# Value products two spots later in the attention loop, opening instructions reordered, and 80 small identity products on TensorE

## The chip, the core and the metric

The kernel runs on one core of a Trainium2 chip. Its engines run side by side, each through its own list of instructions in order, and wait for one another at semaphores: TensorE (PE, matmuls into PSUM), VectorE (DVE), ScalarE (ACT), GpSimd (POOL) and SyncE (SP, which here only issues DMAs). The metric is the device time of one execution in microseconds (us). A profile adds the span of the instructions and the clock that TensorE was granted, 1.00 for 2.4 GHz and 0.50 for 1.2 GHz.

## The reference

Two layers, each with a cross attention and a mixture-of-experts feed-forward, over 8 batches of 128 rows and 256 columns. The change touches the first attention only:

```
x = x + xattn0(layernorm(x), ctx, ctx, encoding, Wq, bq, Wk, bk, Wv, bv, Wm, bm)
  q, k, v = (W @ input + bias) for each batch, 16 heads of 8 channels
  q, k    = rotary(q), rotary(k)            # t * f0 + rotate_half(t) * f1
  prob    = softmax(q k^T / sqrt(8))        # per head, 256 x 256
  out     = Wm @ (prob v) + bm
x = x + ffn0(layernorm(x));  x = x + xattn1(layernorm(x), ctx);  x = x + ffn1(layernorm(x))
```

## The kernel before

**Layout.** In the first attention a "block" b is a batch (NB = 8), and a block has 16 heads, taken as 8 pairs (PAIRS). q and k of a block are split into three bf16 parts, written to DRAM, and read back as "stacks" qstk and kstk, in which both heads of a pair lie one above the other in 64 rows each. The largest score of every row has to be known before the exponentials. So each pair is multiplied twice: once for the row maxima (max_scores, L506, reduced by VectorE at L1175 into mx), and, when the negated maxima have been put into rows of qstk, once more for the exponentials (scores, L527, then ScalarE's Exp at L884 into a prob buffer). pv (L542) multiplies two pairs' prob with the values vt; a block has four such groups (QUADS).

**The way of the maxima.** When the four pairs of a half block are reduced, POOL negates them and splits them into bf16 (negate, six small operations, L1060 to L1064); TensorE transposes them (max_transpose, "maxT", L514), VectorE copies them out (mT, L1179), and SP sends them into qstk (L410).

**The way of q and k.** For block b+3, project (L491) makes q and k; VectorE multiplies with the rotary table (factors, "rope", L1164). Then POOL adds the two (rotate, L337), ScalarE copies the first bf16 part (L891), POOL subtracts (rest, L340), ScalarE copies the second part (L895), POOL makes the third (third, L343), and SP writes and reads back the stacks. POOL's list in block b is: divide(b-1), negate of (b+1, first half), rotate, rest, normalize(b+4), third, negate of (b+1, second half).

**The order.** A block has 16 "spots", two for each pair. All engines follow the same written order: a_uses(b, spot) lists what uses the shared PSUM banks misc(u) in a spot. Even spots hold scores for the next pair and max_scores of a pair of block b+1 or b+2 (MAXES). MAXT says where the maxT stand (6 and 14 in most blocks). q stands at spot 1, k at 5, and v+wm (values of the next block, L497, and output of the last one, L550) at 9; pv at 3, 7, 11 and 15. On VectorE flip (transposes the pv bank, pvT, L1189, and takes the reciprocals, L1191) is at spot 1, flip_back (L1198) at 6. POOL's divide (L1085) stands between the two. In block 7 VectorE also computes the statistics of the next layernorm between flip and flip_back.

**The banks.** misc(u) is one of three banks in turn: max_scores takes two, every other use one. A use may start when the use three banks back has been read (misc_free). exp_buf holds two pairs of scores, prob has three buffers, and pv's bank is one, which flip must have read (pv_free) before the first pv of the next block.

**The opening.** PROLOGUE is the written order before block 0: k and q of blocks 0 to 2, the maxima of block 0, its first maxT. TensorE there waits for the first stacks to come from DRAM (stack_in). VectorE's statistics of blocks 2 to 7 (norm_stats, bn_stats L1150) stand behind q of block 1.

## Time and profile before

| | us |
|---|---|
| median of 3 runs | 462.84 |
| lowest, highest | 459.05, 464.03 |
| the profiled execution | 462.08 |
| its span | 460.3 |
| TensorE busy, VectorE busy | 368.5, 325.0 |
| ScalarE busy, POOL busy | 175.2, 65.9 |
| mean granted clock | 0.915 |

The span is the time from the first to the last instruction of the profiled execution, and 1.8 us lie around it. Busy time is summed over stages that have different limits, so the rows below are read stage by stage. A row of the timeline holds one or several equal instructions; the bracket at its end is the idle time of the engine before it, and what ended that.

### The profile page before, as it was taken

To read this page: it belongs to the slowest core of one execution; us is meant where nothing else is said; L and a number is where in the kernel's file an instruction comes from. 1 tells how busy PE (TensorE), PEld (TensorE's weight loads), DVE (VectorE), ACT (ScalarE), POOL (GpSimd) and SP (SyncE) were. 2 spreads that over 40 slices of the span, in tenths; PEclk is the share of its full clock that TensorE was granted. 3 is DMA by queue.
4 is the path that set the end of the run, shared out by engine and by line. 5 is a ranking of instruction groups with operands and counts; after the bars stand their busy time and mean duration, and the time that the engine had idled before them with its cause. 6 is when DMAs were issued, how large, how long until landed. Compare 5 with 4: busy or idle time off the path is not lost.

```text
span 460.3 us, 7585 instructions
## 1 busy us (share of the span) xinstructions
PE 368.5 (80%) x2754; PEld 221.3 (48%) x2754; DVE 325.0 (71%) x890; ACT 175.2 (38%) x237; POOL 65.9 (14%) x154
## 2 busy tenths in 40 slices
PE   3264888887776669999999999999777887396895
PEld 3122434443343233666666676666455555253453
DVE  5886788989887654674555357677877667869684
ACT  1102456655656512334333334343444444342001
POOL 1214344644422000000000000110011111100000
PEclk9855799999999889999999999999989778976999
DMA  7482366786520400000000000505045444630011
GB/s 244 136 257 69 94 202 160 228 246 216 153 71 19 147 0 0 1 0 2 0 0 1 0 0 3 160 15 146 0 140 155 143 115 129 187 99 0 1 47 46
DMA packets 62371, 41.81 MB, mean 91 GB/s; under 512 B 3968, under 2 KB 60160, under 8 KB 62336
## 3 DMA queue, kind: packets, MB, share of 16 engines
q1 hardware_dynamic: 58240, 34.55, 25.6%
q10 hardware_dynamic: 4096, 6.79, 4.6%
q8 instruction: 22, 0.36, 0.4%
q14 instruction: 13, 0.11, 0.1%
HBM read 26.71 MB, written 14.42 MB: 89 GB/s over the span
## 4 chain that ended last, share of the span: by engine, by line
PE 51%; DVE 33%; issue 7%; POOL 4%; ACT 2%; DMA 2%; DVEq 0%; ACTq 0%; POOLq 0%
PE psum L644 14%; PE psum L631 14%; DVE mx L1175 7%; PE psum L719 4%; PE psum L491 3%; PE psum L619 3%; DVE rope_ab L1164 2%; PE psum L542 2%; DVE stats L1150 2%; PE psum L506 2%; PE psum L757 2%; DVE rs_a L1139 2%; DVE rs_a L1138 1%; PE psum L827 1%; PE psum L843 1%
## 5 line engine op out<-in xcount | busy, mean ns | idle before, releaser
L1175 DVE TENSOR_REDUCE mx<-psum 128x2 f32<-128x512 f32 x128 | 81.1, 683 | 12.8 <-PE psum L506 11.4
L884 ACT ACTIVATE prob<-psum 128x1024 f32<-128x1024 f32 x64 | 63.9, 1022 | 48.7 <-PE psum L527 48.7
L1380 DVE SCALAR_TENSOR_TENSOR xall<-psum,comb,xall 128x256 f32<-128x256 f32 x128 | 53.1, 478 | 41.5 <-PE psum L644 41.1
L644 PE MATMUL psum<-wdn,act 128*128 128x256 f32 x320 | 75.5, 379 | 0.7 <-DVE xall L1377 0.7
L631 PE MATMUL psum<-xnT,wup 128*128 128x512 f32 x160 | 75.6, 596 | 0.0
L644 PEld LDWEIGHTS psum<-wdn,act 128*128 128x128 f32 x320 | 60.7, 190 | 25.9 <-issue 19.1
L946 ACT ACTIVATE rel<-psum 128x512 f32<-128x512 f32 x40 | 23.9, 597 | 95.5 <-PE psum L631 95.5
L343 POOL TENSOR_TENSOR parts<-qk_rest,parts 128x512 bf16<-128x512 f32 x15 | 17.3, 1156 | 226.0 <-ACT parts L972 223.4
L506 PE MATMUL psum<-kstk,qstk 64*128 64x256 bf16 x256 | 27.8, 299 | 22.3 <-DVE mx L1175 12.1
L1002 ACT ACTIVATE prob<-psum 128x1024 f32<-128x1024 f32 x32 | 32.6, 1024 | 25.4 <-PE psum L741 25.4
L542 PE MATMUL psum<-prob,vt 128*32 128x256 f32 x512 | 36.7, 399 | 5.8 <-ACT prob L884 4.7
L631 PEld LDWEIGHTS psum<-xnT,wup 128*128 128x128 f32 x160 | 29.9, 192 | 22.3 <-issue 20.6
L506 PEld LDWEIGHTS psum<-kstk,qstk 64*128 64x128 bf16 x256 | 9.9, 98 | 35.7 <-DVE mx L1175 23.6
L527 PE MATMUL psum<-qstk,kstk 64*128 64x256 bf16 x256 | 25.4, 284 | 0.6 <-DMA qstk<-mT 0.5
L948 ACT ACTIVATE act<-rel 128x512 f32<-128x512 f32 x40 | 25.2, 630 | 1.3
L757 PE MATMUL psum<-prob,vt 128*32 128x128 f32 x512 | 24.5, 321 | 0.2 <-ACT prob L1002 0.2
L542 PEld LDWEIGHTS psum<-prob,vt 128*32 128x32 f32 x512 | 16.5, 112 | 14.5 <-ACT prob L884 6.2
L619 PE MATMUL psum<-eye,xn 128*128 128x128 f32 x48 | 11.9, 341 | 9.7 <-DVE xn L1158 8.1
L827 PE MATMUL psum<-wd,xnT 128*128 128x512 f32 x32 | 16.9, 677 | 2.8 <-DVE xall L1421 2.8
L527 PEld LDWEIGHTS psum<-qstk,kstk 64*128 64x128 bf16 x256 | 8.5, 96 | 21.6 <-issue 13.7
L757 PEld LDWEIGHTS psum<-prob,vt 128*32 128x32 f32 x512 | 14.4, 124 | 7.6 <-issue 5.0
L741 PE MATMUL psum<-qstk,kstk 64*128 64x128 bf16 x256 | 13.6, 232 | 4.4 <-issue 2.4
(156 smaller groups left out, 469.1 us busy)
## 6 DMA issues: line engine op xcount, KB each, us to landing
qstk<-stack_scratch SPq DMA_DIRECT2D x32, 256.0 KB, 4.1
kstk<-stack_scratch SPq DMA_DIRECT2D x30, 256.0 KB, 4.5
stack_scratch<-parts SPq DMA_DIRECT2D x31, 192.0 KB, 2.1
stack_scratch<-parts SPq DMA_DIRECT2D x33, 128.0 KB, 2.1
wup<-in_wup ACTq DMA_DIRECT2D x4, 640.0 KB, 4.8
wdn<-in_wdn ACTq DMA_DIRECT2D x4, 640.0 KB, 5.9
stack_scratch<-parts SPq DMA_DIRECT2D x33, 64.0 KB, 1.9
out<-xall SPq DMA_DIRECT2D x8, 128.0 KB, 1.7
```

Of the source, the lines that this page charges most:

```text
L506: last = nc.tensor.matmul(banks[s][:, nb * D:(nb + 1) * D], qstk[par][rows, pair, nb * P:(nb + 1) * P], kstk[par][rows, pair, :], start=Tr ...
L527: last = nc.tensor.matmul(exp_buf(k)[:, s, mb * D:(mb + 1) * D], kstk[b % SETS][rows, k, mb * P:(mb + 1) * P], qstk[b % SETS][rows, k, :], ...
L542: last = nc.tensor.matmul(pv_bank(1)[32 * j:32 * j + 32, g * D:(g + 1) * D], vt[b % 2][:, mb, 4 * t + j, 8:40] if low else vt[b % 2][:, mb ...
L619: last = nc.tensor.transpose(bank[:, n * P:(n + 1) * P], blk, eye[:])
L631: last = nc.tensor.matmul(psum[:, n % 2, :], wup[:, f, BLOCKS[g], :], xnT[:, f, c * HALF:(c + 1) * HALF], start=(f == 0), stop=(f == 1))
L644: last = nc.tensor.matmul(y_banks(y)[:, j // 2, (j % 2) * D:(j % 2 + 1) * D], act2[n % 2][:, j * P:(j + 1) * P], wdn[:, BLOCKS[g], :], sta ...
L757: last = nc.tensor.matmul(pv_bank(k // 2)[32 * j:32 * j + 32, g * P:(g + 1) * P], v[:, 8 * k + h, 8:40], prob[k % 2][:, at * P:(at + 1) * ...
L884: nc.scalar.activation(prob[(b * PAIRS + k) % 3][:], exp_buf(k).rearrange("p a n -> p (a n)"), ACT.Exp, scale=SCALE).then_inc(exp_done, 1)
L948: nc.scalar.activation(act2[n % 2][:], rel[n % 2][:], ACT.Square).then_inc(a_done, 1)
L1002: nc.scalar.activation(prob[k % 2][:], exp_buf(k).rearrange("p a n -> p (a n)"), ACT.Exp, scale=SCALE).then_inc(exp_done, 1)
L1175: nc.vector.tensor_reduce(mx[:, half, :, 4 * s + p4:4 * s + p4 + 1], bank.rearrange("n (b m) -> n b m", b=2), AX_X, ALU.max).then_inc(misc ...
L1380: last = nc.vector.scalar_tensor_tensor(out=xall[:, b, :], in0=src, scalar=comb[:, b, e:e + 1], in1=xall[:, b, :], op0=ALU.mult, op1=ALU.add)
```

## The change

It has five parts.

1. pv of a group is issued two spots later on TensorE, at spots 5, 9 and 13 and at spot 1 of the next block, and the last one behind the loop. prob has four buffers, since a group's prob is now read later.
2. With it q goes from spot 1 to 3, k from 5 to 7, v+wm from 9 to 11, flip from 1 to 3, flip_back from 6 to 8, and in block 7 the statistics from spot 2 to 3, behind flip as before. MAXES and MAXT stay.
3. The opening's order takes four pairs of maxima ahead of k of block 2 (three before), one between k and q, and the maxT directly behind the sixth. POOL negates the first half ahead of the rotation of q of block 2, not behind it.
4. Four of the six bn_stats of blocks 2 to 7 move into the stretch in which VectorE waits for ScalarE's two copies of block 0.
5. TensorE multiplies the bf16 identity with itself 80 times (WARM) ahead of the first max_scores, into a bank that nobody reads then. The wait for the identity goes from the first projection to this place.

```diff
+WARM = 80
-        prob = [sb(f"prob{i}", [P, 2 * 512]) for i in range(3)]
+        prob = [sb(f"prob{i}", [P, 2 * 512]) for i in range(4)]
...
-            u += [("q", b + 3)] if b + 3 < NB and spot == 1 else []
-            u += [("k", b + 3)] if b + 3 < NB and spot == 5 else []
-            u += [("v+wm", b)] if spot == 9 else []
+            u += [("q", b + 3)] if b + 3 < NB and spot == 3 else []
+            u += [("k", b + 3)] if b + 3 < NB and spot == 7 else []
+            u += [("v+wm", b)] if spot == 11 else []
...
-                    + [("max", 0, n) for n in range(3)] + [("k", 2), ("max", 0, 3), ("q", 2)]
-                    + [("max", 0, 4), ("max", 0, 5), ("maxT", 0, 0), ("max", 0, 6), ("max", 0, 7)])
+                    + [("max", 0, n) for n in range(4)] + [("k", 2), ("max", 0, 4), ("q", 2)]
+                    + [("max", 0, 5), ("maxT", 0, 0), ("max", 0, 6), ("max", 0, 7)])
...
-            pe.wait_ge(eye_in, 32)
...
+                    if use[2] == 0:
+                        pe.wait_ge(eye_in, 32)
+                        for _ in range(WARM):
+                            nc.tensor.matmul(exp_buf(0)[:, 0, 0:P], eye16[:], eye16[:], start=True, stop=True)
...
-                    if spot % 4 == 3:
-                        pv(b, step // 2)
+                    if spot == 1 and b:
+                        pv(b - 1, QUADS - 1)
+                    elif spot % 4 == 1 and spot > 1:
+                        pv(b, spot // 4 - 1)
...
+            pv(NB - 1, QUADS - 1)
...
             normalize(3)
+            negate(PRO_AT["max", 0, 3] + 2, 0)
             rotate(PRO_AT["q", 2] + 1)
             rest(2, 0)
-            negate(PRO_AT["max", 0, 3] + 2, 0)
             third(2, 0)
...
                         add_factors(nc.vector)
+                        dve.wait_ge(x_in[1], 16)
+                        bn_stats_of(FIRST, 2)
                         dve.wait_ge(hi_done, 1)
                         take_rest(nc.vector, 0)
+                        bn_stats_of(FIRST + 2, 2)
                         dve.wait_ge(mid_done, 1)
                         take_third(nc.vector, 0)
...
-                    if spot == 1 and b:
+                    if spot == 3 and b:
                         flip(b - 1)
-                    if spot == 6 and b:
+                    if spot == 8 and b:
                         flip_back(b - 1)
...
-                    if spot == 2 and b == NB - 1:
+                    if spot == 3 and b == NB - 1:
                         norm_stats(0, B_EARLY)
```

VectorE's list from the first maxima of block 2 on (block 2 stands for the blocks 1 to 4; mx are maxima, pvT and den are flip, rope_ab<-psum is first q and then k, o is flip_back). Before:

```order
L1175 TENSOR_REDUCE mx<-psum 128x2 x2
L1189 STREAM_TRANSPOSE pvT<-psum 128x512
L1191 RECIPROCAL den<-pvT 128x32
L1164 SCALAR_TENSOR_TENSOR rope_ab<-psum,cols,rope 128x256 x2
L1175 TENSOR_REDUCE mx<-psum 128x2 x4
L1164 SCALAR_TENSOR_TENSOR rope_ab<-psum,cols,rope 128x256 x2
L1198 STREAM_TRANSPOSE o<-o 128x256
L1175 TENSOR_REDUCE mx<-psum 128x2 x2
L1179 COPY mT<-psum 24x256
```

and after:

```order
L1186 TENSOR_REDUCE mx<-psum 128x2 x4
L1200 STREAM_TRANSPOSE pvT<-psum 128x512
L1202 RECIPROCAL den<-pvT 128x32
L1175 SCALAR_TENSOR_TENSOR rope_ab<-psum,cols,rope 128x256 x2
L1186 TENSOR_REDUCE mx<-psum 128x2 x4
L1190 COPY mT<-psum 24x256
L1175 SCALAR_TENSOR_TENSOR rope_ab<-psum,cols,rope 128x256 x2
L1209 STREAM_TRANSPOSE o<-o 128x256
```

Flip and the two rotary steps now stand one pair of maxima later, and k's stands behind the copy of the transposed maxima.

TensorE's list from the end of block 0 (spot 14) into block 1 (L514 is maxT, L542 pv, L527 scores, L506 max_scores, L491 q). Before:

```order
L514 MATMUL psum<-eye,mpart 24x128 x2
L542 MATMUL psum<-prob,vt 32x256 x8
L527 MATMUL psum<-qstk,kstk 128x256 x4
L506 MATMUL psum<-kstk,qstk 128x256 x4
L491 MATMUL psum<-xn,wa 128x256 x2
L527 MATMUL psum<-qstk,kstk 128x256 x4
```

and after:

```order
L515 MATMUL psum<-eye,mpart 24x128 x2
L528 MATMUL psum<-qstk,kstk 128x256 x4
L507 MATMUL psum<-kstk,qstk 128x256 x4
L543 MATMUL psum<-prob,vt 32x256 x8
L528 MATMUL psum<-qstk,kstk 128x256 x4
L507 MATMUL psum<-kstk,qstk 128x256 x4
L492 MATMUL psum<-xn,wa 128x256 x2
```

The value products went from between maxT and the block's first maxima to between the first and the second.

POOL's list in the opening, from normalize(3) on. Before:

```order
L1073 TENSOR_SCALAR xn<-xall,nmean,rstd 128x256
L337 TENSOR_TENSOR qk<-rope_ab 128x512
L340 TENSOR_TENSOR qk_rest<-qk,parts 128x512
L1060 TENSOR_TENSOR mneg<-zeros,mx 128x16
L1062 TENSOR_TENSOR mpart<-mneg,zeros 128x4x4
```

and after:

```order
L1081 TENSOR_SCALAR xn<-xall,nmean,rstd 128x256
L1068 TENSOR_TENSOR mneg<-zeros,mx 128x16
L1070 TENSOR_TENSOR mpart<-mneg,zeros 128x4x4
L1071 TENSOR_TENSOR mneg<-mneg,mpart 128x16
L1070 TENSOR_TENSOR mpart<-mneg,zeros 128x4x4
```

The negation now stands ahead of the rotation and the rest of q and k of block 2. Inside the loop POOL's list did not move.

## Rows read from the trace of the kernel before

**Rows 1.** Windows: length, busy time (x instructions) of PE, PEld, DVE, ACT, POOL; clock, DMA.

```profile
14.00:18.40 4.40, 0.00 (x0) 0.00 (x0) 3.72 (x9) 0.62 (x1) 0.41 (x1) 1.00 0.66 178
18.50:52.50 34.00, 18.34 (x101) 7.95 (x102) 24.90 (x58) 6.22 (x8) 11.05 (x25) 0.50 0.44 129
...
154.90:158.40 3.50, 1.40 (x20) 0.53 (x20) 3.05 (x15) 2.12 (x3) 0.00 (x0) 1.00 0.79 285
158.50:161.70 3.20, 3.19 (x22) 1.21 (x22) 0.48 (x1) 1.02 (x1) 0.00 (x0) 0.50 0.01 2
```

**Rows 2.** Timeline of the opening: start, duration, engine, line, operation, [idle before].

```profile
13.93 0.69 DVE L340 TENSOR_TENSOR qk_rest<-qk,parts 128x512 f32<-128x512 f32 x1 [0.68 <-ACT parts L891]
...
17.82 2.05 DVE L1150 BATCH_NORM_STATS2 stats<-xall 128x6 f32<-128x256 f32 x6
...
23.76 0.61 PE L506 MATMUL psum<-kstk,qstk 64*128 64x256 bf16 x4 [9.91 <-DMA kstk<-stack_scratch]
...
25.14 4.08 DVE L1175 TENSOR_REDUCE mx<-psum 128x2 f32<-128x512 f32 x6
...
29.99 0.88 DVE L1164 SCALAR_TENSOR_TENSOR rope_ab<-psum,cols,rope 128x256 f32<-128x256 f32 x2 [0.77 <-PE psum L491]
...
38.95 0.37 PE L514 MATMUL psum<-eye,mpart 128*24 128x128 bf16 x2 [3.77 <-POOL mpart L1064]
...
39.36 0.28 DVE L1179 COPY mT<-psum 24x256 bf16<-24x256 bf16 x1 [2.85 <-PE psum L514]
...
41.76 1.04 PE L527 MATMUL psum<-qstk,kstk 64*128 64x256 bf16 x8 [0.49 <-DMA qstk<-mT]
...
43.26 2.69 DVE L1175 TENSOR_REDUCE mx<-psum 128x2 f32<-128x512 f32 x4 [0.66 <-PE psum L506]
```

**Rows 3.** Timeline of VectorE in a middle block.

```profile
78.20 1.29 DVE L1175 TENSOR_REDUCE mx<-psum 128x2 f32<-128x512 f32 x2 [0.89 <-PE psum L506]
79.41 0.70 DVE L1189 STREAM_TRANSPOSE pvT<-psum 128x512 f32<-128x512 f32 x1
...
83.61 0.88 DVE L1164 SCALAR_TENSOR_TENSOR rope_ab<-psum,cols,rope 128x256 f32<-128x256 f32 x2
...
93.39 0.69 DVE L1175 TENSOR_REDUCE mx<-psum 128x2 f32<-128x512 f32 x1 [0.90 <-PE psum L506]
```

**Rows 4.** Timeline of POOL in the same block.

```profile
80.58 0.77 POOL L1085 TENSOR_TENSOR o<-pvT,den 128x128 f32<-128x128 f32 x2 [4.25 <-DVE den L1191]
...
84.57 1.27 POOL L337 TENSOR_TENSOR qk<-rope_ab 128x512 f32<-128x512 f32 x1 [0.38 <-DVE rope_ab L1164]
...
88.55 1.16 POOL L343 TENSOR_TENSOR parts<-qk_rest,parts 128x512 bf16<-128x512 f32 x1 [0.29 <-ACT parts L895]
89.81 0.22 POOL L1060 TENSOR_TENSOR mneg<-zeros,mx 128x16 f32<-128x16 f32 x1
...
91.31 0.22 POOL L1064 TENSOR_TENSOR mpart<-mneg,zeros 128x16 bf16<-128x16 f32 x1
```

**Rows 5.** Timeline of TensorE, same block: scores, maxima's products, k's projection, value products.

```profile
77.55 0.39 PE L527 MATMUL psum<-qstk,kstk 64*128 64x256 bf16 x4
...
77.78 0.38 PE L506 MATMUL psum<-kstk,qstk 64*128 64x256 bf16 x4
...
82.44 1.13 PE L491 MATMUL psum<-ctx_all,wa 128*128 128x256 f32 x4 [0.20 <-DVE mx L1175]
...
91.78 1.03 PE L542 MATMUL psum<-prob,vt 128*32 128x256 f32 x13
```

**Rows 6.** Timeline of block 7 and the loop's end.

```profile
158.51 1.19 PE L550 MATMUL psum<-o,wa 128*128 128x256 f32 x2 [1.99 <-DVE o L1198]
...
164.61 0.72 DVE L1189 STREAM_TRANSPOSE pvT<-psum 128x512 f32<-128x512 f32 x1 [4.38 <-PE psum L542]
```

**Rows 7.** Timeline of TensorE in the second attention: small bf16 products of 128 columns.

```profile
337.24 0.40 PE L741 MATMUL psum<-qstk,kstk 64*128 64x128 bf16 x8
...
343.60 0.61 PE L741 MATMUL psum<-qstk,kstk 64*128 64x128 bf16 x8
```

More of the change, by code:

```diff
@@ L99, in build @@
         mT = sb("mT", [24, 2, D], BF16)
-        prob = [sb(f"prob{i}", [P, 2 * 512]) for i in range(3)]
-        fill = prob[2][:].bitcast(BF16)[:, 0:4 * D].rearrange("p (t r n) -> p t r n", t=2, r=2)
+        prob = [sb(f"prob{i}", [P, 2 * 512]) for i in range(4)]
+        fill = prob[3][:].bitcast(BF16)[:, 0:4 * D].rearrange("p (t r n) -> p t r n", t=2, r=2)
         vt = [sb(f"vt{i}", [P, 2, 16, VROW]) for i in range(2)]
@@ L544, in pv @@
                             vt[b % 2][:, mb, 4 * t + j, 8:40] if low else vt[b % 2][:, mb, 4 * t + j, 0:32],
-                            prob[(b * PAIRS + k) % 3][:, (2 * s + mb) * D:(2 * s + mb + 1) * D],
+                            prob[k % 4][:, (2 * s + mb) * D:(2 * s + mb + 1) * D],
                             start=(low and mb == 0), stop=(not low and mb == 1), skip_group_check=True)
@@ L883, in exps @@
                 act.wait_ge(st_full, b * PAIRS + k + 1)
-                nc.scalar.activation(prob[(b * PAIRS + k) % 3][:], exp_buf(k).rearrange("p a n -> p (a n)"), ACT.Exp,
+                nc.scalar.activation(prob[k % 4][:], exp_buf(k).rearrange("p a n -> p (a n)"), ACT.Exp,
                                      scale=SCALE).then_inc(exp_done, 1)
@@ L1145, in rows_of, with bn_stats_of, norm_stats @@
                 return xall[:, b, :] if isinstance(b, int) else xall[:, bass.ds(b, 1), :].rearrange("p o n -> p (o n)")
-            def norm_stats(first, n):
+            def bn_stats_of(first, n):
                 for b in range(first, first + n):
                     last = nc.vector.bn_stats(stats[:, b, :], xall[:, b, :])
-                steps.then(last)
+                return last
+            def norm_stats(first, n, given=0):
+                steps.then(bn_stats_of(first + given, n - given))
                 for b in range(first, first + n):
@@ L1237, in _ @@
                     if (kind, b) == ("q", 1):
-                        dve.wait_ge(x_in[1], 16)
-                        norm_stats(FIRST, NB - FIRST)
+                        norm_stats(FIRST, NB - FIRST, 4)
                         normalize(2, 0)
```

1 line of the change is left out of this document (added).

## The prediction

> **What bounds the kernel now.** I read the span, then the clock by windows, then the timelines of the three stretches that the change touches: the opening, one middle block of the first attention, and block 7. The profiled execution took 462.08 us, of which 460.3 are span. It is 0.8 under the median of 462.84. My sum is made against the 462.08 and then moved up by half of that distance.
>
> In the opening TensorE idles 9.91 us until the first stacks arrive, and has lost its clock by then: 1.00 until 18.40, 0.50 from 18.50 to 52.50 [rows 1, 2]. VectorE sets the pace after that, with two visible holes: 0.77 before k's rotary step, 2.85 before the copy of the first transposed maxima, which waited for TensorE's maxT, which had waited 3.77 for POOL [rows 2].
>
> In a middle block the maxima of one block begin at 78.20 and those of the next at 93.39, so a period is **15.19 us** [rows 3]; the same row stands at every start of the blocks 1 to 5. VectorE has its largest hole, 0.89 to 0.90, right there: TensorE was held by maxT and then did 1.03 us of value products before the maxima [rows 3, 5]. And maxT waited for POOL, whose last negation ran at 91.31 [rows 4]. Two things meet at POOL's second negation at 89.81: POOL's own third part, 88.55 + 1.16 = 89.71, and VectorE's maxima of the pair, which end at the same time. So two chains of equal length bound a block: VectorE's work, and the way from k's rotary step through POOL and ScalarE back to POOL.
>
> **The middle blocks.** I lay the new order out with the durations of the rows, from one kend (k's rotary step has given VectorE free, 83.61 + 0.78 = 84.39) to the next.
>
> - kend to maxT of the second half. The work is unchanged: rotate at 84.57, first copy, rest, second copy, third, six negations up to 91.31 + 0.22, and maxT at 91.67 [rows 4]. That is **7.3 us**. What stood beside it has shrunk: between k's rotary step and the second negation VectorE had flip_back, three pairs of maxima, one mT and the output (5.35 us); now k comes a pair later and has flip_back and two pairs in front of it (2.9 us). The tie is broken, and POOL alone is the bound by 2.3 us.
> - maxT to the block's first maxima: before 93.39 - 91.67 = 1.72, with the value products in between. Now they are gone from there, so 1.72 - 1.03 = **0.7**. This is the gain that the change has in a block.
> - first maxima to the second: the value products stand here now. TensorE is free 0.31 after it starts the maxima's products (77.78 to the next at 78.09), the value products take 1.03, scores 77.78 - 77.55 = 0.23, and from the maxima's products to VectorE's start it is 78.20 - 77.78 = 0.42 [rows 3, 5]; less the 0.42 that it is ahead that is **1.6**, where a pair of maxima alone takes VectorE 1.25.
> - the second maxima themselves: **1.25**.
> - flip to k. Flip starts at 79.41 and POOL's divide at 80.58, 1.17 later; divide takes 0.77 [rows 3, 4]. Before, flip was a pair of maxima earlier than the end of the second pair, and the first negation waited for those maxima, not for divide. Now it stands behind divide: 1.17 + 0.77 + 0.1 + 1.72 (six negations) + 0.14 = 3.9 to maxT. k's projection is queued behind maxT on TensorE and needs 83.61 - 82.44 = 1.17 [rows 3, 5], k's rotary step 0.78: **5.9**. VectorE's own work in this stretch (flip, q, two pairs, mT, k: 5.4) hides all but 0.5.
>
> Sum 7.3 + 0.7 + 1.6 + 1.25 + 5.9 = **16.7 us** against 15.19, or +1.5 in each of four blocks (1 to 4, which have a q and a k): **+5.9**. The bounds of one block: if a step beside POOL is shorter than I lay it (0.5 of the k wait, 0.3 of the second maxima), +0.7; if ScalarE's second copy, which is behind the values of the next block in its queue, comes late, +2.1. Block 5 and 6 have no k and POOL is not their bound; the same walk gives +0.1 and +0.5. The fourth prob buffer takes a wait from nobody: ScalarE's Exp waits for scores, never for pv.
>
> **The opening.** Four of six bn_stats leave the queue in front of the first maxima, 4/6 of 2.05 = 1.4 us [rows 2]. They go into waits for ScalarE of 0.68 each (one row of two stands in the group) and take 0.68 each, so they cost the stacks' way 0.1. The first maxima then start when TensorE's products are there, some 0.7 after 23.76, at 24.5 in place of 25.14: -0.7. The early negation takes the 2.85 hole away: POOL may negate when the fourth pair is reduced (29.9), ready at 31.7, long before TensorE comes to maxT at 34.2. With cold durations (a projection starts 2.1 before its rotary step, 27.88 to 29.99, and a pair of maxima takes 4.08 / 3 = 1.36) I get mT at 36.0 against 39.36, the row operands 2.4 later as before (41.76 - 39.36), and block 1's first maxima of the loop at 39.7 against 43.26 [rows 2]: -3.6. In block 0 the new order gives half a us back, as k comes a pair later: with the value products at half clock (twice 1.03) and the clock back at about 49 us, kend is at 52.0, and block 1 begins at 52.0 + 7.3 + 0.7 = 60.0. Before it was 78.20 - 15.19 = 63.0. So the opening brings **-3.0**; if the clock comes back only at 52.5 as before, -1.6.
>
> **The 80 products.** TensorE is idle when they run, so they cost nothing unless they last beyond 23.76. The nearest row has eight 128-column products of bf16, two at a time, in 0.40 less the 0.07 of overlap, 41 ns each, and in 0.61 with a cold clock, 68 ns [rows 7]. One at a time would be at most twice that. So 80 take between 3.3 and 6.6 us with the clock at 1.00, and end between 17.2 and 20.5; only cold would they last to 24.8 and cost 1.0. What they keep is the question. From their end to the stacks TensorE again has 3.3 to 6.6 us of nothing. In block 7 the clock fell at 158.4 after a stretch of 3.5 us in which TensorE had worked 1.40 [rows 1], and the first products of the opening are as thin: 0.4 at full clock for each 1.3 us of VectorE. I count **0**, with bounds of 0 and -5.0, which is the same walk with all durations at full clock (block 1 at 55.0).
>
> The Trainium skill, "TensorE: Matmul & The Clock Gate", Part 1, says that TensorE's clock is throttled by default, is released by sustained activity and goes back when the engine idles, for which the section on oscillation has a wait for DMA between bursts as the example. By the first half of it the 80 products would bring the warm walk; by the second they would bring nothing. The same page gives 56 ns from one such product to the next on a warm array, by which, as an estimate, they would take 4.5 us.
>
> **Block 7 and the loop's end.** Here the shift helps. TensorE waits for o of block 6 (output at 158.51, behind VectorE's statistics), and had only reached spot 9 [rows 6]. Now it reaches spot 11 before it waits, so scores of pair 6 and a group of value products are done, and behind the output come pair 7's scores, Exp and two groups. To the last flip I get 4.5 to 5.4 us in place of 164.61 - 158.51 = 6.1; less the +0.5 by which block 6 comes later: **-0.6**, bounds -1.6 and +0.5. What follows is unchanged.
>
> **Sum.** 462.1 + 5.9 + 0.1 - 3.0 - 0.6 = 464.5, and with half the distance to the median **465 us**.
>
> **The rivals.**
>
> *The clock holds through the opening.* For it: nothing but the 80 products differs in the 10 us in which it fell. Against it: the gap that is left, and the thin work after it. It gives 465 - 5 = 460.
>
> *The loop is bound by VectorE, not by POOL.* Then flip and k a pair later do not matter, and only the hole of 0.9 goes: 15.19 - 0.9 in four blocks, or -3.6 in place of +5.9, 455.5. For it: VectorE is the busiest engine of the block and has the hole. Against it: the tie at 89.8, and POOL's chain, of which no step was moved forward.
>
> *ScalarE's queue makes the chain longer; this one ends slower.* The copy of the values (behind v+wm, now at spot 11) stands ahead of the second part's copy. In my walk the values are full at kend + 2.9 and rest is done at kend + 3.3. Once v+wm comes more than 0.4 us late, each further us is paid in each block. At +0.6, the chain is 17.3, +8.3 in all, which with the opening's lower bound of -1.6 gives 469.
>
> **How the numbers follow.** Forecast 0.52, its own range 461 to 468. The held clock 0.13, VectorE's bound 0.13, ScalarE's queue 0.22. About 1%, 4.6 us, is what a measurement of this kernel can tell from no change (its three runs lie 5 us apart). Faster than 458.2: all of VectorE's rival and a third of the clock's, 0.18. Slower than 467.5: most of ScalarE's rival (0.17) and the forecast's upper tail (0.09), 0.26. Within: 0.56. The range is 456.5 to 469.5, which leaves out half of VectorE's rival and some of the slow one.
>
> **What would show it.** Right: the block starts lie 16.7 apart, maxT waits for POOL's mpart at both halves, VectorE idles before k's rotary step and before mT; the first maxima start at 24.5 and the clock is 0.50 again from before 27; the last flip comes 5 us after the output of block 6. Wrong: block starts 14.3 apart (the chain through POOL was no bound), or a clock of 1.00 between 25 and 45.

## The result, and the profile after

The changed kernel takes **470.32 us** (median of four runs, 469.51 to 471.15), the kernel before 463.16 (459.05 to 464.03). The ratio is 1.0173, with a 95% interval of 1.0109 to 1.0237: slower by 1.7%, where the prediction had 465.0 and a range of 456.5 to 469.5. The profiled execution took 469.51, its span is 467.6, against 460.3 before. Some executions of several kernels, the kernel before among them, took from one per cent to several times longer than their fellows: the ratios below leave these out, the medians keep them, and the profile of the run with the weights in blocks 4 to 7 is of such an execution.

The span is laid out below by the starts of the first maxima of each block's pair 2 (the row that opens [rows 3]) and by the last two flips (pvT). All times in us.

| stretch | before | after | difference | forecast |
|---|---|---|---|---|
| start to block 1's first maxima | 63.00 | 57.15 | -5.85 | -3.0 |
| block 1 | 15.20 | 16.66 | +1.46 | +1.5 |
| block 2 | 15.19 | 17.92 | +2.73 | +1.5 |
| block 3 | 15.20 | 19.90 | +4.70 | +1.5 |
| block 4 | 15.20 | 17.87 | +2.67 | +1.5 |
| block 5, and block 6 to flip(6) | 27.47 | 27.87 | +0.40 | +0.6 |
| flip(6) to flip(7) | 13.35 | 11.83 | -1.52 | -1.1 |
| flip(7) to the end | 295.7 | 298.4 | +2.7 | 0 |

Block 1 is the block that I had laid out, and it is right to 0.1. Blocks 2 to 4 together take 5.7 more than three blocks like block 1; that is the loss that the prediction did not have.

The windows of the changed kernel, as in [rows 1]:

```profile
14.00:18.40 4.40, 3.20 (x33) 3.21 (x34) 4.13 (x21) 0.00 (x0) 1.27 (x1) 0.67 0.57 157
...
22.00:25.50 3.50, 1.14 (x12) 0.30 (x12) 3.10 (x6) 0.00 (x0) 1.43 (x2) 1.00 1.09 322
25.50:45.50 20.00, 14.78 (x76) 6.47 (x80) 15.28 (x28) 4.92 (x6) 7.52 (x21) 0.51 0.43 128
46.00:73.40 27.40, 20.99 (x248) 10.59 (x242) 21.71 (x41) 15.47 (x19) 12.91 (x28) 1.00 0.55 159
73.50:76.50 3.00, 3.00 (x28) 1.03 (x24) 1.29 (x2) 1.31 (x2) 0.00 (x0) 0.50 0.86 226
...
100.40:104.90 4.50, 4.21 (x30) 2.08 (x32) 3.19 (x8) 0.34 (x1) 1.22 (x1) 0.62 0.70 189
111.50:114.80 3.30, 3.30 (x28) 1.46 (x27) 1.63 (x3) 1.50 (x2) 0.00 (x0) 0.55 0.87 232
```

The first thing to see is the last three rows: the granted clock, which before stayed at 1.00 through the middle blocks, falls three times in the loop, once in each of the blocks 2, 3 and 4. In the opening it is 0.67 on average in 14.0 to 18.4, under the first of the 80 products, then 1.00 for three pairs of maxima (until 25.5), down for 20 us, and back at 46, not at 52.5.

The opening's timeline, as in [rows 2]:

```profile
15.20 6.26 PE L576 MATMUL psum<-eye 128*128 128x128 bf16 x80 [2.15 <-DVE rope_ab L1175]
...
21.96 0.39 PE L507 MATMUL psum<-kstk,qstk 64*128 64x256 bf16 x4 [0.50 <-DMA kstk<-stack_scratch]
22.40 4.96 DVE L1186 TENSOR_REDUCE mx<-psum 128x2 f32<-128x512 f32 x8 [1.36 <-PE psum L507]
28.25 0.88 DVE L1175 SCALAR_TENSOR_TENSOR rope_ab<-psum,cols,rope 128x256 f32<-128x256 f32 x2 [0.89 <-PE psum L492]
32.22 0.39 PE L515 MATMUL psum<-eye,mpart 128*24 128x128 bf16 x2 [0.43 <-DVE rope_ab L1175]
33.28 0.27 DVE L1190 COPY mT<-psum 24x256 bf16<-24x256 bf16 x1
35.67 1.03 PE L528 MATMUL psum<-qstk,kstk 64*128 64x256 bf16 x8 [0.24 <-DMA qstk<-mT]
37.17 5.49 DVE L1186 TENSOR_REDUCE mx<-psum 128x2 f32<-128x512 f32 x8 [0.41 <-PE psum L507]
```

The first stacks' products start 1.80 earlier, at 21.96 and not at 23.76; maxT no longer waits 3.77 for POOL; block 1's first maxima are at 37.17, where I had 39.7. One reason for the earlier stacks is a row of the kernel before that I had not weighed, the first projection at the program's start:

```profile
7.83 2.08 PE L491 MATMUL psum<-ctx_all,wa 128*128 128x256 f32 x4 [2.10 <-DMA eye<-in_eye]
```

The same product starts at 5.65 in the changed kernel, since the wait for the identity went to its first user. It is not the whole story: in the profiles of two later runs with the same opening the stacks' products start at 23.08 and 23.70, so that 1.80 is what this execution shows and not a fixed gain.

A middle block, as in [rows 3 to 5]: here block 1 of the changed kernel, the sound one, from maxT to k's rotary step and on to the next maxT.

```profile
56.29 0.27 PE L515 MATMUL psum<-eye,mpart 128*24 128x128 bf16 x2 [1.48 <-POOL mpart L1072]
...
57.15 1.29 DVE L1186 TENSOR_REDUCE mx<-psum 128x2 f32<-128x512 f32 x2 [0.27 <-PE psum L507]
...
58.69 1.29 DVE L1186 TENSOR_REDUCE mx<-psum 128x2 f32<-128x512 f32 x2 [0.25 <-PE psum L507]
59.90 0.71 DVE L1200 STREAM_TRANSPOSE pvT<-psum 128x512 f32<-128x512 f32 x1
...
65.04 0.88 DVE L1175 SCALAR_TENSOR_TENSOR rope_ab<-psum,cols,rope 128x256 f32<-128x256 f32 x2 [0.78 <-PE psum L492]
...
72.51 0.22 POOL L1072 TENSOR_TENSOR mpart<-mneg,zeros 128x16 bf16<-128x16 f32 x1
...
72.88 0.27 PE L515 MATMUL psum<-eye,mpart 128*24 128x128 bf16 x2 [1.48 <-POOL mpart L1072]
...
73.70 1.93 PE L543 MATMUL psum<-prob,vt 128*32 128x256 f32 x16
```

TensorE idles 1.48 before maxT, where it idled 0.70 before. And from 73.5 on the value products take 1.93, where they took 1.07: the clock fell right behind this hole. It does not fall behind each of them: the same 1.48 stands at 56.29 and at 90.87, and the clock stayed. In block 3 something else is added. TensorE and the queues that issue transfers (SPq of SyncE, ACTq of ScalarE):

```profile
90.77 2.74 SPq L374 DMA_DIRECT2D stack_scratch<-parts  x3
90.87 0.27 PE L515 MATMUL psum<-eye,mpart 128*24 128x128 bf16 x2 [1.48 <-DVE mx L1186]
...
91.52 0.55 ACTq L923 DMA_DIRECT2D wup<-in_wup  x1
...
92.09 1.42 ACTq L924 DMA_DIRECT2D wdn<-in_wdn  x1
...
93.55 0.77 SPq L411 DMA_DIRECT2D qstk<-mT  x1
...
99.29 0.40 PE L528 MATMUL psum<-qstk,kstk 64*128 64x256 bf16 x4 [2.93 <-DMA qstk<-mT]
```

Pair 4's scores wait 2.93 for the rows of negated maxima (mT), which SP issued at 93.55, behind both halves (wup and wdn) of a chunk of the inner weights. In the kernel before it is the other way round in every block (by 0.2 to 0.5 us), and TensorE needs the rows only 7.03 after maxT (91.67 to 98.70); now it would take them 5.5 after it (90.87 to 96.36):

```profile
92.96 0.77 SPq L410 DMA_DIRECT2D qstk<-mT  x1
93.18 0.57 ACTq L915 DMA_DIRECT2D wup<-in_wup  x1
...
93.78 0.94 ACTq L916 DMA_DIRECT2D wdn<-in_wdn  x1
...
98.70 0.39 PE L527 MATMUL psum<-qstk,kstk 64*128 64x256 bf16 x4
```

In the changed kernel the weights go first in all four blocks, 0.5 ahead of the rows in blocks 1, 2 and 4, and yet TensorE waits there only 0.20, 0.32 and 0.23. In block 1 the rows were there 4.5 after their issue. In blocks 2 and 4 they took 6.0 and 6.1, longer than in block 3, but the clock had just fallen, and TensorE came to pair 4 only 6.8 and 7.0 after maxT. Block 2 of the changed kernel:

```profile
74.05 0.76 SPq L411 DMA_DIRECT2D qstk<-mT  x1
...
80.04 0.39 PE L528 MATMUL psum<-qstk,kstk 64*128 64x256 bf16 x4 [0.32 <-DMA qstk<-mT]
```

So a fall of the clock right behind maxT hides that the rows are late. In block 3 it did not fall there, the wait stands open, and the clock falls behind the wait (0.62 in 100.4 to 104.9).

Block 7, as in [rows 6], and the small products, as in [rows 7]:

```profile
164.62 0.67 PE L551 MATMUL psum<-o,wa 128*128 128x256 f32 x2 [3.25 <-DVE o L1209]
...
169.20 0.72 DVE L1200 STREAM_TRANSPOSE pvT<-psum 128x512 f32<-128x512 f32 x1 [3.38 <-PE psum L543]
...
335.51 0.40 PE L749 MATMUL psum<-qstk,kstk 64*128 64x128 bf16 x8
```

From the output of block 6 to the last flip it is 4.58 in place of 6.10. The layers behind the loop then begin with the clock down for longer (0.55 in 172.0 to 179.6, against 0.78 in the stretch that lies as far behind the last flip before, 167.4 to 175.0), and the first chunk, L639 to L652, takes 4.95 in place of 3.74. The small product of [rows 7] is as before.

### The profile page after: what moved, and what is told of

Read it like the earlier page. It is cut to its first block, busy times and chain, and to the rows that moved or that the text cites. A ratio compares the mean times of both kernels' runs of the same rounds, so it can differ in the third digit from the quotient of the medians.

```text
span 467.6 us, 7744 instructions
## 1 busy us (share of the span) xinstructions
PE 382.2 (82%) x2834; PEld 229.5 (49%) x2834; DVE 324.8 (69%) x890; ACT 174.4 (37%) x237; POOL 65.8 (14%) x154
## 4 chain that ended last, share of the span: by engine, by line
PE 52%; DVE 27%; issue 6%; POOL 5%; DMA 4%; ACT 3%; SPq 1%; DVEq 0%; POOLq 0%
PE psum L639 14%; PE psum L652 13%; DVE mx L1186 4%; PE psum L727 4%; PE psum L543 4%; PE psum L627 3%; PE psum L492 2%; PE psum L528 2%; PE psum L507 2%; DMA qstk<-mT 2%; DVE stats L1157 1%; DVE rs_a L1147 1%; DVE rs_a L1146 1%; PE psum L765 1%; DVE pvT L1438 1%
## 5 line engine op out<-in xcount | busy, mean ns | idle before, releaser
L1186 DVE TENSOR_REDUCE mx<-psum 128x2 f32<-128x512 f32 x128 | 81.3, 683 | 17.2 <-PE psum L507 16.5
L639 PE MATMUL psum<-xnT,wup 128*128 128x512 f32 x160 | 76.8, 604 | 0.0
L652 PE MATMUL psum<-wdn,act 128*128 128x256 f32 x320 | 75.5, 379 | 0.7 <-DVE xall L1390 0.7
L652 PEld LDWEIGHTS psum<-wdn,act 128*128 128x128 f32 x320 | 60.7, 190 | 25.9 <-issue 19.2
L344 POOL TENSOR_TENSOR parts<-qk_rest,parts 128x512 bf16<-128x512 f32 x15 | 17.4, 1158 | 230.3 <-ACT parts L980 227.4
L639 PEld LDWEIGHTS psum<-xnT,wup 128*128 128x128 f32 x160 | 30.4, 195 | 23.0 <-issue 21.4
L543 PE MATMUL psum<-prob,vt 128*32 128x256 f32 x512 | 38.3, 423 | 3.0 <-ACT prob L892 1.7
L528 PE MATMUL psum<-qstk,kstk 64*128 64x256 bf16 x256 | 26.4, 288 | 6.8 <-DMA qstk<-mT 3.9
L543 PEld LDWEIGHTS psum<-prob,vt 128*32 128x32 f32 x512 | 15.4, 118 | 17.3 <-issue 10.7
L899 ACT CAST parts<-qk 128x512 bf16<-128x512 f32 x8 | 5.0, 619 | 42.5 <-POOL qk L338 30.3
L507 PEld LDWEIGHTS psum<-kstk,qstk 64*128 64x128 bf16 x256 | 11.0, 100 | 18.2 <-DVE mx L1186 14.7
L1175 DVE SCALAR_TENSOR_TENSOR rope_ab<-psum,cols,rope 128x256 f32<-128x256 f32 x32 | 13.5, 466 | 6.9 <-PE psum L492 6.9
```

The costliest lines, as they stand in the source:

```text
L507: last = nc.tensor.matmul(banks[s][:, nb * D:(nb + 1) * D], qstk[par][rows, pair, nb * P:(nb + 1) * P], kstk[par][rows, pair, :], start=Tr ...
L528: last = nc.tensor.matmul(exp_buf(k)[:, s, mb * D:(mb + 1) * D], kstk[b % SETS][rows, k, mb * P:(mb + 1) * P], qstk[b % SETS][rows, k, :], ...
L543: last = nc.tensor.matmul(pv_bank(1)[32 * j:32 * j + 32, g * D:(g + 1) * D], vt[b % 2][:, mb, 4 * t + j, 8:40] if low else vt[b % 2][:, mb ...
L639: last = nc.tensor.matmul(psum[:, n % 2, :], wup[:, f, BLOCKS[g], :], xnT[:, f, c * HALF:(c + 1) * HALF], start=(f == 0), stop=(f == 1))
L652: last = nc.tensor.matmul(y_banks(y)[:, j // 2, (j % 2) * D:(j % 2 + 1) * D], act2[n % 2][:, j * P:(j + 1) * P], wdn[:, BLOCKS[g], :], sta ...
L1186: nc.vector.tensor_reduce(mx[:, half, :, 4 * s + p4:4 * s + p4 + 1], bank.rearrange("n (b m) -> n b m", b=2), AX_X, ALU.max).then_inc(misc ...
```

## The experiments

Each ratio is to the kernel before, run on the same chip, with its 95% interval. Totals are medians of 4 to 10 executions, everything else is read from the one profiled execution of a run. "Flips" are the starts of pvT; the kernel before has them 15.19 apart in blocks 1 to 4, the changed kernel 17.94, 16.64, 21.19 and 16.58.

### Which part

**Loop alone, opening alone.** The order of the loop (spots of q, k, v+wm, flips; value products late; four prob buffers) on the old opening, and the new opening with the old loop:

```diff
-                    if spot % 4 == 3:
-                        pv(b, step // 2)
+                    if spot == 1 and b:
+                        pv(b - 1, QUADS - 1)
+                    elif spot % 4 == 1 and spot > 1:
+                        pv(b, spot // 4 - 1)
...
-            u += [("k", b + 3)] if b + 3 < NB and spot == 5 else []
+            u += [("k", b + 3)] if b + 3 < NB and spot == 7 else []
```

> The kernel before with parts 1 and 2 alone (value products and the steps with them two spots later, four prob buffers); the opening is the old one. If the loop's longer way through POOL, and what follows from it, is the cause, the blocks 1 to 4 take 16.7 to 20 us each as after the change, and the time is 8 to 12 us over before, 471 to 475. If the loss comes from the opening or from the 80 products, it is within 2 us of before and the block starts lie 15.2 apart.

> The changed kernel with parts 1 and 2 undone (three prob buffers, all spots as before); new opening, 80 products, wait for the identity moved. By my ledger of the two traces the opening gives 5.9 us at the first maxima of block 1, of which some 1.8 is the wait for the identity that no longer stands ahead of the first projection: 457 to 458, block starts 15.2 apart. If the new opening only shifts which wait is last, it is within 2 us of before.

The loop alone took 471.36, ratio 1.0168 (1.0108 to 1.0228), with flips 18.12, 16.55, 20.21 and 16.55 apart: the whole loss. The opening alone took 459.49 (before 462.93), ratio 0.9959 (0.9924 to 0.9995), with flips 15.19 apart. Its flip(0) is at 57.51 against 64.21, 6.7 earlier, and nothing is lost behind it: from flip(7) to the end are 295.7 in both profiles. But the profiled execution, 455.66, is the fastest of the ten. The 6.7 belongs to it; in the total the opening gives 1.9 by the ratio, with an interval of 0.2 to 3.5, and 3.4 by the medians.

**One move of the loop at a time.** First the value products late and all else at its old spot, then the other way round.

> The changed kernel with q, k, v+wm, flip, flip_back and the statistics back at their old spots; only the value products stay two spots later. If k's place is what lengthens the way through POOL, a block takes 7.3 + 0.7 + 7.1 = 15.1 us and the time is 455 to 457 (the opening's 5.9, 0.4 in the blocks, 1 in block 7). If late value products themselves are the loss, the blocks take over 16 us and the time stays above 465.

> Changed kernel, but with the value products back where they were (ahead of the block's first maxima, three prob buffers): only q, k, v+wm, flip and flip_back come a pair later. Theory of the prediction's walk (k's projection and rotary step, now behind the divide and the negation, set the period): the walk gives 7.3 + 1.72 + 1.25 + 1.25 + 5.9 = 17.4 us for a block, with late rows on top in some; loop loses 9 us, total 467 to 473. Rival (the late value products are what costs, as with them alone in the third kernel, 16.48): flips 15.2 to 15.9 apart, total 459 to 463.

The value products late and all else in its place: 464.18, ratio 1.0035 (1.0004 to 1.0066), flips 16.5 apart (16.8 in block 3), where the walk had 15.1. k's projection now stands behind a group of value products, and its rotary step waits 0.76 for it; ScalarE's second copy stands behind that of the values, and POOL waits 1.3 to 1.8 for it. The granted clock is 1.00 from 54 to 150 in this kernel, with holes of at most 0.7 ahead of maxT. The other move alone, late spots with the value products where they were, is far worse, 505.65, ratio 1.0936 (1.0854 to 1.1017), flips 24.7 to 26.1 apart, which neither theory had (17.4 and 15.2 to 15.9). The rows show a piece of the reason; VectorE, then TensorE:

```profile
88.17 0.71 DVE L1197 STREAM_TRANSPOSE pvT<-psum 128x512 f32<-128x512 f32 x1
...
88.97 1.94 PE L543 MATMUL psum<-prob,vt 128*32 128x256 f32 x16 [2.06 <-issue]
...
92.95 0.88 DVE L1172 SCALAR_TENSOR_TENSOR rope_ab<-psum,cols,rope 128x256 f32<-128x256 f32 x2 [3.69 <-PE psum L492]
```

The next block's first value products stand at spot 3 and write the bank that the late flip reads, so TensorE stands still until the flip, with the maxima's products behind it. (The profile calls this wait "issue"; that it is for the flip follows from the written order and from the flip's end at 88.88.) The late spots need the late value products. The reverse does not hold: with the value products alone late the kernel is 6 faster than with both. How much of the 10 us per block is this wait and how much the clock (0.50 in 84 to 92) was not taken apart.

### Why blocks 2 to 4 are longer than block 1

**Filled holes.** Twelve products of the identity ahead of each of nine maxT:

```diff
+                    if 2 <= b <= 5 or (b, use[2]) == (1, 1):
+                        for _ in range(HOLD):
+                            nc.tensor.matmul(bank[:, 0:P], eye16[:], eye16[:], start=True, stop=True)
                     pe.wait_ge(neg_done, 2 * b + use[2] + 1)
```

> The changed kernel with 12 more products of the identity ahead of nine maxT of the blocks 1 to 4 (and the last of block 0), where TensorE waits for POOL; they take 0.94 us each time and lie in waits of 0.94 and 1.48. If the falls of the clock in the loop (73.5, 100, 111.5) cost what I read off the blocks 2 and 4, these two come back from 17.9 to 16.7, and the time is 2.5 to 4 us under the changed kernel's 470.3. If the clock is no cause and the periods have another reason, nothing changes or it is slower.

471.37, ratio 1.0174 (1.0086 to 1.0262). The rows were late in all four blocks (1.58, 2.84, 2.33, 1.74), and the clock fell behind those waits (0.55 in 82 to 89). In block 2:

```profile
77.35 0.91 SPq L412 DMA_DIRECT2D qstk<-mT  x1
83.07 0.61 PE L529 MATMUL psum<-qstk,kstk 64*128 64x256 bf16 x4 [2.84 <-DMA qstk<-mT]
```

This is what hid the fillers' gain. In each of the four blocks the rows were there 5.7 to 6.1 after their issue, as in blocks 2 to 4 of the changed kernel, but with the clock held TensorE was there earlier and waited. The clock alone was not the cause, and holding it could not show what it costs.

**Rows issued ahead of the writes of q's and k's parts,** without and with the fillers:

```diff
                 rows_at(b + 1, 0)
-                parts_to_dram(b + 3)
                 rows_at(b + 1, 1)
+                parts_to_dram(b + 3)
```

> The changed kernel with one edit on SP: the DMA of the second half's negated maxima into qstk is issued ahead of the six writes of the parts of q and k, not behind them. If the wait of TensorE for these rows (2.93 us at 99.3 in block 3, 0.2 to 0.3 in the others) and the fall of the clock behind it are the second part of the loss, block 3 comes from 19.9 to 17 to 18 and the time to 466 to 468. If the rows are late for another reason (the weights' transfers on the DMA engines), the wait stays and so does 470.

> The same, with the 12 identity products ahead of the maxT of the blocks 1 to 4 as in e4. If e4 lost because the rows' wait (1.6 to 2.8 us in four blocks there) grew and took the clock with it, and the clock is otherwise a cost, now all four blocks take 16.7 and the time is 463 to 466. If the fillers themselves cost, it is above e5.

470.22, ratio 1.0168 (1.0080 to 1.0257), and 469.81, ratio 1.0146 (1.0054 to 1.0239). Without the fillers the rows' waits shrank to 0.42, 0.15 and 0.82, and a wait for the stacks, now written later, took their place in block 2:

```profile
91.25 0.39 PE L507 MATMUL psum<-kstk,qstk 64*128 64x256 bf16 x4 [2.00 <-DMA kstk<-stack_scratch]
```

With the fillers the clock was 1.00 from 93 to 152 and the waits remained (3.2 us in all for stacks, 2.6 for rows), so a held clock with transfers late gives next to nothing, again.

**The weights elsewhere.** Chunks of inner weights in blocks 4 to 7 instead of 1 to 4; then all four at the end of block 7 (the second edit is shown):

```diff
-                    if 1 <= b <= 4 and k == 1:
-                        inner_weights(CHUNK * (b - 1))
+                    if b == 7 and 4 <= k <= 7:
+                        inner_weights(CHUNK * (k - 4))
```

> The changed kernel with the loads of the feed-forward's weights (1.3 MB in each of the blocks 1 to 4, from ScalarE's queue at pair 1) moved to the blocks 4 to 7. If the late rows (2.93 us in block 3) and, with SP's order turned, the late stacks are the DMA engines' being full of weights, the waits for DMA in the loop go, with them the fall of the clock at 100, and the blocks 2 to 4 come to 16.7 to 17: 464 to 467. If SP's queue alone is late, the waits and 470 stay. At 4.9 us in all under the change, what is left over before is the way through POOL.

> Changed kernel, but the four chunks of the inner weights are issued at the end of block 7 (Exps 4 to 7) instead of in blocks 1 to 4, so that no large transfer runs beside the blocks 1 to 6. Theory (late rows come from the weights' transfers, and the falls of the clock from the holes): flips of blocks 1 to 4 all 16.5 to 16.7 apart, TensorE waits at most 0.3 for mT's rows, granted clock 1.00 from 50 to 150; flip(6) is some 5 us earlier than in the changed kernel. The layers behind the loop then wait for their weights, so the total is no measure of the loop; I expect 468 to 480. Rival (the loop loses its clock because TensorE's work is thinner, whatever the transfers do): at least one block of 17.5 or more, with 0.50 in its windows.

In blocks 4 to 7 the loss did not go: 471.5, ratio 1.0172 (1.0134 to 1.0210). In the profile blocks 1 and 2, now without weights, are 16.56 and 16.57 with no late rows, and rows are late at 119.07 and 137.56 (2.35 and 1.68), where the weights now are. The times from this profile are an indication only, and nothing below rests on them.

With no weights in the loop the flips are 16.63, 16.59, 18.15 and 16.58 apart, and no wait for rows is left. My theory's first half holds, its second (a clock of 1.00) does not: as the rival has it, one block is long by the clock alone. The windows of it:

```profile
106.00:108.00 2.00, 0.73 (x12) 0.31 (x8) 1.45 (x3) 2.00 (x3) 1.69 (x6) 1.00 0.19 54
108.00:110.00 2.00, 1.51 (x14) 0.73 (x18) 0.92 (x3) 0.90 (x2) 0.26 (x2) 0.70 0.97 292
110.00:112.00 2.00, 2.00 (x22) 0.83 (x16) 0.99 (x2) 0.29 (x1) 0.00 (x0) 0.50 0.18 51
```

TensorE worked 0.73 of the 2 us before 108, maxT is at 108.48, and soon behind it TensorE has half its clock; that costs 1.55. (The total, 473.95, ratio 1.0256, 1.0197 to 1.0314, has a wait of 9.17 for wdn behind the loop and says nothing of the loop.)

**The same weights in the same blocks, 3 us later,** and that with the fillers:

```diff
-                    if 1 <= b <= 4 and k == 1:
+                    if 1 <= b <= 4 and k == 3:
                         inner_weights(CHUNK * (b - 1))
```

> Changed kernel, but ScalarE issues each chunk of the inner weights behind the block's Exp 3 instead of Exp 1, that is about 3 us later in the same blocks 1 to 4, so that mT's row operands go out ahead of them. Theory (the rows wait because in the changed kernel they are issued behind the weights, 93.55 against 91.52 and 92.09, where before they were issued ahead, 92.96 against 93.18 and 93.78): TensorE's waits for the rows are at most 0.3 in each block, the flips lie 16.6 apart but for a block with a fall of the clock (18.2), total 465 to 468. Rival (any transfer of that size in the block delays the rows or the stacks): waits of 1 us or more for rows or stacks remain, total 469 to 472.

> The kernel with the weights behind the rows, and 12 products of the identity on TensorE ahead of each of the nine maxT of the loop (the idle 1.48 us are filled). Theory: with the rows in time and the clock held the four blocks are 16.6 to 16.9 apart (the fillers may delay maxT by 0.1 to 0.2), granted clock 1.00 from 50 to 150, total 464 to 467. Rival (the clock falls for other holes, or the fillers delay maxT by more, as with the fillers alone): a period over 17.5 in at least one block, total 468 to 472.

467.02, ratio 1.0109 (1.0068 to 1.0150), flips 16.56, 16.56, 18.12 and 16.54 apart, no wait for rows or stacks. In block 3:

```profile
91.00 2.91 SPq L374 DMA_DIRECT2D stack_scratch<-parts  x3
...
93.95 0.77 SPq L411 DMA_DIRECT2D qstk<-mT  x1
...
94.87 0.56 ACTq L923 DMA_DIRECT2D wup<-in_wup  x1
...
96.50 0.39 PE L528 MATMUL psum<-qstk,kstk 64*128 64x256 bf16 x4
```

SP issues the rows as late as in the changed kernel (2.9 behind maxT, there 2.7), and they are there 2.55 later, without a wait; behind the weights they took 5.74. So it is the weights ahead of them that make the rows late, and not SP's queue.

With the fillers 460.98, ratio 0.9953 (0.9910 to 0.9995), flips 16.55 apart in all four blocks. TensorE's waits of that kernel from 50 to 150 us (engine, line, releaser: us in total, times, longest) and a window of it:

```profile
PE psum L516 <- POOL mpart L1076: 3.0, 5, 0.6
PE psum L529 <- ACT prob L896: 3.0, 10, 0.6
...
108.00:112.00 4.00, 3.81 (x44) 1.99 (x46) 3.10 (x7) 2.07 (x3) 0.13 (x1) 1.00 0.54 165
```

So both rivals of these two runs fell, and the excess of the blocks 2 to 4 is accounted for: it is the order of weights and rows together with the clock. Moving the weights alone took 4.6 of it away (the four periods are 67.8 long, 72.4 in the changed kernel); holding the clock alone took nothing. The total of the last kernel is 3 lower than my theory had it (464 to 467), and where that comes from is open; see below.

### The opening

> e2 (new opening, old loop) without the 80 products. If they only burn idle time, the first maxima of the loop lie where e2 has them, within 0.5 us. If they hold the clock over the first three maxima as the trace after the change shows (1.00 until some 25.5), and bring its return forward, it is 1 to 3 us slower than e2.

> The kernel before with the wait for the identity moved from the first projection to the first maxT, and nothing else. My sum left this out. If TensorE's wait of 2.1 us there set the way to the first stacks, these arrive 1.5 to 2 us earlier and the time is 1 to 2 us under before; if another wait takes its place, nothing.

```diff
-            pe.wait_ge(eye_in, 32)
             for use in PROLOGUE[1:]:
...
                 elif kind == "maxT":
+                    pe.wait_ge(eye_in, 32)
                     pe.wait_ge(neg_done, 1)
```

The identity's wait alone, on the kernel before: 460.28, ratio 0.9972 (0.9919 to 1.0024), flip(0) at 61.94 against 64.21, so 2.3 at block 1. The whole new opening on the old loop, with 0 products in place of 80: 457.80, ratio 0.9850 (0.9717 to 0.9982), flip(0) at 59.50, the lowest median of all kernels here. Read from the profiles, the three steps to flip(0) are -2.3 for the identity, -2.4 for the statistics, the early negation and the order of the opening, and -2.0 for the products. None of the three is shown by that. Kernels that up to flip(0) differ in the place of the weights' issue alone (56.9 or later) lie as far apart there, from one profiled execution to another: 59.90, 61.57 and 62.29 in the changed kernel and in those with the weights 3 us later and behind the loop, 61.46 and 58.39 in two kernels of the next section on one chip. Only the sum, 6.7, is larger than this spread. The products' 2.0 is not seen in the medians either (459.49 with them, on another chip), and the next pair of kernels has it the other way.

What the 80 products take depends on the clock that they meet. In five profiles it is 0.50 for some 3 us of their time, and they take 6.12 to 6.27; in eight it is 1.00 throughout, and they take 4.64:

```profile
15.69 4.64 PE L577 MATMUL psum<-eye 128*128 128x128 bf16 x80 [2.68 <-DVE rope_ab L1179]
```

In all thirteen the clock is 0.50 again by 30 at the latest, though in three it comes back once for some 3 us.

### Is there a better late order

> e3 (only the value products late), and in the spots 5, 9 and 13 TensorE does k, v+wm before the value products, not behind them. In e3 k's rotary step stood at 98.20 behind 1.03 us of value products, and ScalarE's second copy at 103.72 behind v+wm, 1.4 after the rest was there, so that the way from k to maxT was 8.6 in place of 7.3. If these two are why e3 takes 15.75 a block and not 15.1, a block takes 14.3 to 14.6 now, under the 15.19 of before, and the time is 456 to 459. If the value products late cost something else, it stays over 15.5 and at 462 to 464.

> e10 without the 80 products. The two runs of the opening alone differed by 2.0 us at block 1 for the products, and the other way round in the time (459.5 with, 457.8 without, intervals that overlap). If the products bring 2 us, this is 2 us over e10; if the end takes them back, the same or less.

> e10 with the weights' loads late as in e9. If the DMA engines bound nothing in e10, no change; if rows or stacks come late there, 1 to 3 us less.

```diff
                     elif spot % 4 == 1:
+                        for use in a_uses(b, spot) if spot > 1 else []:
+                            a_use(use, misc(A_AT[use]), A_AT[use])
                         if spot > 1:
                             pv(b, spot // 4 - 1)
```

With late value products, old spots, and k and v+wm ahead of the value products of their spot, the flips are 15.87 apart in all three, not 14.3 to 14.6, and the totals 461.96, 459.98 and 463.55 (ratios 0.9990, 0.9974 and 1.0019, with 1 inside every interval). In the expectation I wrote that the kernel with the value products alone late takes 15.75 a block; its trace has 16.5. The hole ahead of the block's first maxima is down from 0.89 to 0.31, and others are there instead:

```profile
86.92 1.16 POOL L344 TENSOR_TENSOR parts<-qk_rest,parts 128x512 bf16<-128x512 f32 x1 [0.74 <-ACT parts L906]
...
87.49 2.48 DVE L1189 TENSOR_REDUCE mx<-psum 128x2 f32<-128x512 f32 x4 [0.59 <-PE psum L507]
```

POOL waits 0.74 for a copy that ScalarE made behind that of the values, where it waited 0.29 [rows 4]. My theory of a shorter block fell; which of the small waits makes the 0.7 was not taken apart. Of the first two, which ran on the same chip and differ in the products alone, the one without them has its flip(0) at 59.67 and the one with them at 61.46, with a clock of 0.89 and 0.50 in 30 to 34. The third, with the products again, has it at 58.39.

## Why the prediction was wrong

- **The step that failed is the sum of the middle blocks, "+5.9"**: it measured +11.6. (Its five terms add up to 16.75 a block, which would have been +6.2.) For the order that it was made for, the walk held. Block 1 of the changed kernel is 16.66 against 16.7: first to second maxima 1.54 (1.6), second maxima 1.21 (1.25), flip to k's end 5.92 (5.9), k's end to maxT 7.06 (7.3), maxT to the first maxima 0.93 (0.7). With both other causes removed all four blocks are 16.55, or +5.4. The other 6 or so come from what the walk took for constant: that mT's rows land in time, and that TensorE has its clock. Used for other orders the walk failed: 15.1, 17.4 and 14.3 to 14.6 forecast, 16.5, 25 and 15.87 measured. In those the wait for ScalarE's second copy, the bank of the value products and the clock come in, so the walk describes this order and is no model of the loop.
- **Late rows.** I had checked no transfer of the middle blocks. With the new order pair 4's scores come 5.5 behind maxT and no longer 7.03, and the rows' issue stands behind a chunk of weights. With the weights behind the rows the total fell from 470.32 to 467.02, on other chips (ratios 1.0173 and 1.0109, intervals that overlap); in the trace the wait of 2.93 is gone.
- **The clock.** I weighed it in the opening and in block 7, and not in the loop, although the walk itself says that POOL alone bounds the block and TensorE then waits. The hole ahead of maxT grew from 0.70 to 1.48, and the clock fell behind it in some blocks. One fall costs 1.55. Filling it, with the rows in time, gave 6 us (467.02 to 460.98, same chip; the intervals are apart). The two profiles explain only part of that. The kernel without fillers has the fall in block 3 and another ahead of flip(0) (0.50 in 57 to 60), which delays the second maxima by 1.2; from flip(7) to the end it takes 298.2 and the other 294.8. That last difference is not near the edit: 180 us behind flip(7) the two are level to 0.1, and it arises in 346 to 415, with a clock of 0.83 in one and 0.90 in the other in 350 to 400. Whether the fillers bring it is not shown.
- **The opening, "-3.0"**, measured -5.85. The identity's wait of 2.10 stood in the kernel before and I gave it no term; without it the first projection starts 2.2 earlier, and alone it brought flip(0) 2.3 forward in one profile (in the total, ratio 0.9972, not clear of nothing). The first maxima start at 22.40, where I had 24.5, and the clock is back at 46, where I had 49. But -5.85 is partly the luck of the profiled execution: with the same opening block 1's first maxima stand at 57.66 to 59.40 in six other profiles, 5.3 to 3.6 ahead of the kernel before, and the clock is back between 46 and 51. The term was too small by somewhere between 0.6 and 2.9.
- **The 80 products, "0".** They took 6.26 us here, partly at half clock, and 4.64, 58 ns each, where the clock was 1.00: inside the 3.3 to 6.6. Of what they keep the runs say 2.0 for and 1.8 against, and two profiles of the same opening lie 3.1 apart; 0 stands as well as any number.
- **Block 7, "-0.6"** with the +0.5 of block 6: measured -1.52 and about +0.35. Output to flip took 4.58, inside the 4.5 to 5.4. What the sum left at 0, the layers behind the loop, has +2.7, of it 1.2 in their first chunk at half clock. The same instructions take 292.9 to 299.3 in the profiles of these kernels, so the 2.7 cannot be put down to the change.
- **The rivals.** The held clock did not come: 0.51 from 25.5 to 45.5, as the forecast had it (0.50 from before 27). VectorE as the bound (14.3 a block) is refuted by the 16.55. ScalarE's queue gave about the right total, 469, by a mechanism that is not there: k's end to maxT is 7.06, not longer than the 7.3 of the walk. It shows only in the kernels with old spots, there with 1.3 to 1.8 and 0.74 of wait in front of POOL's third part.

The Trainium skill, "TensorE: Matmul & The Clock Gate", section "A second HAM failure mode: psum-queue depth-cycling", describes a kernel in which frequent short idle times between groups of products, with no wait for a transfer, make the clock go to and fro. Here the trace agrees: the fall at 73.5 stands behind a hole of 1.48 with no transfer late. The same page's Part 1 gives the 56 ns from which the prediction had 4.5 us for the 80 products; the traces with a clock of 1.00 agree, at 4.64. Its section "Back-to-back issue gap" gives about 81 ns for each of a stream of weight loads with products of 128 columns. Each of the 80 has its weight load, and at full clock they take 58 ns; where the page and the measurement differ, the measurement decides.

## What to carry over

When a reorder leaves one engine as the sole bound, walk the others too: list what TensorE now idles per block and whether the clock survived such a hole anywhere in the trace, and for each small transfer compare the time from issue to need, and who is issued ahead of it. A reorder can swap two queues' issues without touching either queue. When two causes overlap, one can hide the other: here a fallen clock gave late rows the time to land, and with the clock held they were waited for. Removing one alone can then show nothing; try them together before dropping either. And before a difference between two profiles is read as an effect, look how far two profiles of the same instructions lie apart; here that was 3 us at the loop's start and 6 in the layers behind it.

## What was not expected of the hardware

- The transfer of 12 KB of rows was waited for until 5.7 to 6.1 us after its issue where the first of two weight transfers of 640 KB had been issued 0.5 to 2.0 ahead of it (seven blocks of two kernels, 4.5 in an eighth), and was there within 2.55 where the weights were issued 0.9 behind it.
- SP's issue of three writes took 2.74 in block 3 where it takes 1.44 in other blocks. The weights' issues that run beside it from 91.52 are not the reason: with them moved to 94.87 it took 2.91. The cause is open.
- Twelve idle-filling products (0.84 us) ahead of each of nine maxT kept a clock of 1.00 from 54 to 150, at no cost in the block's period (16.55 with them, 16.56 without). With rows late they did not keep it.
- Eighty products of 128 columns, each with its weight load, took 4.64 us at a clock of 1.00.
